# ScalarE's exponential ahead of its PSUM copies, and GpSimd's index copies split in pairs, in a graph network kernel

## The reference, cut to what matters

```
z = (x @ W).reshape(N, H, F)
e = leaky_relu(el[src] + er[dst], 0.2)
m = segment_max(e, dst)
ex = exp(e - m[dst])
s = segment_sum(ex, dst)
out = segment_sum(z[src] * (ex / s[dst]), dst) + b
```

## Time and profile before

| | us |
|---|---|
| median of 3 runs | 7727.45 (7714.45 to 7744.26) |
| the profiled execution | 7731.27 |
| its span, first to last instruction | 7729.6 |
| PE busy | 4457.3 |
| DVE busy | 4150.8 |
| ACT busy | 2129.1 |
| POOL busy | 3270.2 |

### The profile page before, as it was taken

The page is one execution under the profiler, slowest core; times in us unless marked ns, Lnnn a source line. Parts: engine busy times, 40 slices in busy tenths (PEclk is TensorE's granted clock), DMA queues, the critical chain, the costliest instruction groups (busy, mean ns, idle before and its releaser), DMA issues.

```text
span 7729.6 us, 118765 instructions
## 1 busy us (share of the span) xinstructions
PE 4457.3 (58%) x28553; PEld 2928.7 (38%) x28553; DVE 4150.8 (54%) x13273; ACT 2129.1 (28%) x5938; POOL 3270.2 (42%) x3549
## 2 busy tenths in 40 slices
PE   1455555555555565344444444444477988888865
PEld 1223333223233235122222222222256767676754
DVE  3566676767676663455655565556574111223344
ACT  0344444444444441133333233333320000000000
POOL 3666666656565612666666666656600000000000
PEclk9666766666776665566666666666667999999988
DMA  5454454545444532344444444444437989899976
GB/s 88 112 144 134 136 145 131 145 129 145 136 143 134 143 113 49 97 111 122 121 112 121 121 121 116 120 110 123 120 108 287 416 340 416 345 416 401 373 291 260
DMA packets 934339, 1390.68 MB, mean 180 GB/s; under 512 B 483496, under 2 KB 689474, under 8 KB 917769
## 3 DMA queue, kind: packets, MB, share of 16 engines
q1 hardware_dynamic: 687776, 912.42, 35.0%
q0 software_dynamic: 128976, 222.12, 11.6%
q10 hardware_dynamic: 117332, 253.47, 8.8%
HBM read 1014.16 MB, written 373.27 MB: 179 GB/s over the span
## 4 chain that ended last, share of the span: by engine, by line
issue 18%; SPq 16%; PE 14%; another core or an unknown queue 13%; DVE 13%; DMA 13%; ACT 7%; DVEq 4%; ACTq 2%
DMA arena<-adj_w_d 8%; ACT arena L1889 4%; DMA arena<-adj_c_d 4%; SPq L498 4%; SPq L519 4%; PE bank L1754 3%; PE bank L1755 2%; PE bank L1758 2%; SPq L485 2%; DVE arena L1018 2%; PE bank L1716 2%; SPq L500 2%; PE bank L1610 1%; DVE arena L1041 1%
## 5 line engine op out<-in xcount | busy, mean ns | idle before, releaser
L798 POOL DMA_INDIRECT arena<-table_d,arena x3136 | 3093.4, 986 | 1956.7 <-issue 974.0
L1610 PE MATMUL bank<-arena 128*128 128x500 f16 x3750 | 1351.9, 497 | 1312.4 <-issue 720.1
L1631 PE MATMUL bank<-arena 128*65 128x40 f32 x7500 | 649.0, 257 | 1053.8 <-ACT arena L1949 538.8
L1610 PEld LDWEIGHTS bank<-arena 128*128 128x128 f16 x3750 | 430.2, 122 | 2026.1 <-issue 1798.0
L1889 ACT ACTIVATE arena<-arena 128x128 f16<-128x128 f16 x3750 | 1126.6, 392 | 239.1 <-DVEq L1119 133.0
L1631 PEld LDWEIGHTS bank<-arena 128*65 128x65 f32 x7500 | 618.0, 171 | 1174.0 <-issue 611.6
L1754 PE MATMUL bank<-arena 125*128 125x250 f16 x3750 | 857.9, 274 | 156.2 <-DMA arena<-adj_w_d 132.9
L1018 DVE TENSOR_SCALAR arena<-arena 128x500 f16<-128x500 f16 x1875 | 681.7, 364 | 411.5 <-issue 207.2
L1755 PE MATMUL bank<-arena 125*128 125x250 f16 x3750 | 853.9, 273 | 0.0
L1612 PE MATMUL bank<-arena 128*128 128x500 f16 x1875 | 695.7, 474 | 203.6 <-issue 200.1
L1104 DVE SCALAR_TENSOR_TENSOR arena<-arena,bank 128x250 f16<-128x250 f16 x1250 | 455.8, 412 | 559.2 <-ACT arena L1913 297.8
(11 more groups left out here) (244 smaller groups left out, 4244.8 us busy)
## 6 DMA issues: line engine op xcount, KB each, us to landing
arena<-adj_w_d SPq DMA_DIRECT2D x720, 625.0 KB, 10.8
arena<-adj_c_d SPq DMA_DIRECT2D x345, 625.0 KB, 11.4
adj_w_d<-arena ACTq DMA_DIRECT2D x125, 1250.0 KB
arena<-msg_d SPq DMA_DIRECT2D x1250, 103.5 KB
msg_d<-arena POOLq DMA_DIRECT2D x196, 552.0 KB
adj_c_d<-arena ACTq DMA_DIRECT2D x125, 625.0 KB
arena<-table_d,arena POOLq DMA_INDIRECT x3136
arena<-in_edge_features SPq DMA_DIRECT2D x625, 51.0 KB
```

The costliest lines, as they stand in the source:

```text
L798: g_.indirect_dma_start(ring[:, i, k * XC:(k + 1) * XC], None, table_d, bass.IndirectOffsetOnAxis(ap=idx_cur[:, i, k:k + 1], axis=0)).then ...
L1610: mm(wb, lhsT=row_oh[:, slot, c, i, :], rhs=col_oh[:, slot, c, :], start=(c == 0 and i == 0), stop=(c == CH - 1 and i == 1))
L1631: last = mm(out, lhsT=rows_sl[:, g, w, c, 0:AGG], rhs=grh[:, g, w * CH + c, :], start=(c == 0), stop=(c == CH - 1))
```

## The change

In `blocks_pool` the copy of a block's 16 indices becomes 8 copies of two indices, each after the pace wait of its pair and ahead of its two gathers, with a wait for each. In `win_scalar` the wait for `logits_made`, the exponential and its wait come ahead of `finish(g-1)`, and the copies of the first window due go behind that and behind the issue of the maxima's store.

```diff
-                g_.tensor_copy(idx_cur[:, i], row_idx[:, bass.ds(j * BK, BK)]).then_inc(s("idx_here"), 1)
-                wait_reg(pool, s("idx_here"), j + (layer * NBLK + 1))
                 for k in range(BK):
-                    if place is not None and k % 2 == 0:
-                        wait_reg(pool, s("dve_step"), place + k * PER_BLOCK // BK)
+                    if k % 2 == 0:
+                        if place is not None:
+                            wait_reg(pool, s("dve_step"), place + k * PER_BLOCK // BK)
+                        g_.tensor_copy(idx_cur[:, i, k:k + 2], row_idx[:, bass.ds(j * BK + k, 2)]).then_inc(s("idx_here"), 1)
+                        wait_reg(pool, s("idx_here"), j * (BK // 2) + (layer * NBLK * (BK // 2) + k // 2 + 1))
                     g_.indirect_dma_start(ring[:, i, k * XC:(k + 1) * XC], None, table_d, bass.IndirectOffsetOnAxis(
                         ap=idx_cur[:, i, k:k + 1], axis=0)).then_inc(gathered[i], 16)
@@
                     evacuate(b, todo[0] - 1)
+                    act.wait_ge(s("logits_made"), b * NG + (ng + g + 1))
+
+                    wait_some(act, s("win_psum"), b * NG + (ng + g - NG + 1))
+                    act_(flat(grh[:, g]), flat(gd[:, g % GS]), ACT.Exp).then_inc(s("exp_made"), 1)
                     if not (first(b) and g == 0):
                         finish(b if g else b - 1, (g - 1) % NG)
-                    evacuate(b, todo[0])
-                    act.wait_ge(s("logits_made"), b * NG + (ng + g + 1))
-
-                    wait_some(act, s("win_psum"), b * NG + (ng + g - NG + 1))
-                    act_(flat(grh[:, g]), flat(gd[:, g % GS]), ACT.Exp).then_inc(s("exp_made"), 1)
                     act.dma_start(max_d[:, bass.ds((b * NG + g) * (WG * WH), WG * WH)], top_b[0:1, g % 2, 0:WG * WH]).then_inc(top_stored[g % 2], 16)
-                    for n in todo[1:-1]:
+                    for n in todo[:-1]:
                         evacuate(b, n)
```

More of the change, by code:

```diff
@@ L1942, in win_scalar @@
                     evacuate(b, todo[0] - 1)
-                    if not (first(b) and g == 0):
-                        finish(b if g else b - 1, (g - 1) % NG)
-                    evacuate(b, todo[0])
                     act.wait_ge(s("logits_made"), b * NG + (ng + g + 1))
@@ L1949, in win_scalar @@
                     act_(flat(grh[:, g]), flat(gd[:, g % GS]), ACT.Exp).then_inc(s("exp_made"), 1)
+                    if not (first(b) and g == 0):
+                        finish(b if g else b - 1, (g - 1) % NG)
                     act.dma_start(max_d[:, bass.ds((b * NG + g) * (WG * WH), WG * WH)], top_b[0:1, g % 2, 0:WG * WH]).then_inc(top_stored[g % 2], 16)
-                    for n in todo[1:-1]:
+                    for n in todo[:-1]:
                         evacuate(b, n)
```

## The result

The changed kernel takes 7837.3 us (7831.4 to 7843.7) against 7726.9 for the kernel before on the same chip: a ratio of 1.0142, with a 95% interval of 1.0123 to 1.016. It is 110 us slower, where 7680 and 47 us faster was forecast. The profiled execution took 7843.7 us, its span is 7842.0.

The account below looks back on a forecast made before the run. Held signals stretch the VectorE, ScalarE and TensorE loop; after the change GpSimd bounds it. 98 x 26.9 plus a 40 us tail gives 2676 us a stage, -47 and 0, so 7684 profiled, 7680 us median; range 7540 to 8000.

Parts of the forecast that it names:

- What bounds the kernel now: Loop of VectorE, ScalarE and TensorE, stretched by signals held during long gather rows: 21.8 us a group against 17.7 unheld.
- Part one: ScalarE's exponential moved ahead of finish(g-1): taken at -100 us alone, bounds -540 to +250, worth 0 in the sum.
- Part two: GpSimd's index copies in pairs: 5 us more work a block, 26.9 us in all, making GpSimd the bound.
- a tenth up: Upper bound for GpSimd's gap with a copy, 0.1 us above the 1.00 taken: 7840 us.
- The cover: GpSimd's idle time absorbs the added copies: 26.9 us of work a block against 26.8 us taken before.
- The tail: From a stage's last gather to its last logits: 40 us, against 96 and 77.5 before.
- Rival (a): Pauses of 1.0 us free nothing, so signals stay held and the loop slows: 8120 us, chance 0.25.
- The row at 4869.51: In a long gather row, a copy gives 1.08 us without a gather, yet L1910 starts only at 4880.40.
- the row of two gathers: Trace example at 4543.30: after two gathers, the late L1932 starts 0.85 us after the last gather's end.
- Rival (b): GpSimd's pair is 0.1 to 0.2 us cheaper than the rows say: 7400 to 7550 us, chance 0.12.
- Rival (c): Holds come from something other than gathers and GpSimd isn't bound; part one alone pays: 7630 us, chance 0.08.
- The signs: Expected profile marks: 26.9 us a block, VectorE waiting for msg_d, L1932's waits far under 1523 us, tail near 40 us.

Follow-up runs that it names:

- pairs alone: The kernel before with its index copies made two at a time and ScalarE's old order kept: 7817.8 us, ratio 1.011.
- fours: The changed kernel with indices copied four at a time ahead of four gathers: 7218.5 us, ratio 0.9335.
- eights with the long pause: The changed kernel with indices copied eight at a time, each copy made four times over with waits between: 7369.1 us, ratio 0.9552.
- the three forms that ran: The changed kernel with indices copied eight at a time, that copy made two, three or four times over: 7057.8, 7203.4 and 7350.8 us.

## Why the prediction was wrong

**What bounds the kernel now.** Right, and shown: no signal is held over 1.27 us with a quarter of the gathers, nor with memsets for the others, and behind rows of eight a longer pause alone frees them. How the gathers hold them is open. It holds for chips of the slow kind; that the stretch depends on the chip was in no row of the trace that I had.

**Part one.** Right for the sum (its value in it was 0, and pairs alone, 7817.8 us, are within 20 us of both parts). Alone it gives 50 us where 100 was taken. Its bounds, -540 to +250, were far too wide.

**Part two, the step that failed.** "So a block takes 26.9 us when GpSimd never waits." It takes 27.74, so that GpSimd, the bound as forecast, is slower than the 26.8 and 26.5 us of the kernel before and not level with them. The form of the sum is right and its terms are too low by 0.83 us a block: the gathers 16 x 1.010 = 16.16 us against 15.92, 0.24 more; the gaps with a copy, up to 2 us, average 1.014 against 1.00, 0.11 more; the gaps without one average 0.383 with the stores in them, 3.06 us a block against 2.99, 0.07 more; and the 47 gaps over 2 us average 2.72, (2.72 - 1.00) x 47 / 196 = 0.41 more. That is 0.84 x 196 = 164 us; with tails 13 us shorter than taken and 8 us outside the stages it is the 159 us between 7684 and 7843.7. I had taken undisturbed rows for the gap, and a mean of gathers from a kernel in which GpSimd idles a fifth of the time. The mean gather is 986 ns in the kernel before, 997 with fours, 1002 with pairs alone and 1010 in the changed kernel; that the copies and VectorE's traffic stretch it is only argued. The long gap once in four blocks can't be seen in a kernel without eight copies a block; fours have none at that place, and its cause is open. Of the bounds, "a tenth up" for the gap gave 7840, which is where the time came out, but by other terms.

**The cover.** "26.9 against 26.8" left no room: each tenth of a microsecond that the block was underpriced went to the end, 20 us. Forecasting the likelier side from a difference smaller than the error of its terms was the weak point, more than any one row.

**The tail** was taken at 40 us and is 36.6 and 30.6.

**Rival (a)**, that holds stay: it didn't come, and neither did its condition, a pause freeing fewer than one signal in three: behind two gathers it frees 92%. The row at 4869.51 that spoke for it stood behind a long row, and the row of two gathers that spoke against it was the one that carried over. The delay from the start of the aggregate's last matmul to its signal has a median of 0.5 us in the changed kernel and 5.6 in the kernel before; the longest are 4.9 and 35.7, and 3 to 10 us were forecast for the longest holds. **Rival (b)**, the cheaper pair: no, the pair costs more. **Rival (c)**, holds from another source: no, by the two runs with a quarter of the gathers.

**The signs.** VectorE's wait for `msg_d`, L1932's and L1949's waits, the missing pace waits and GpSimd's share came as written, and the gap between pairs is 1.014 us on average (1.07 with the 47 long ones), inside 0.9 to 1.1; VectorE's wait for L1914, L1913 before, is 13.6 us in all, so that part one costs nothing there. Only the block's 26.9 us did not come.

## What to carry to other kernels

An engine's idle time can be what frees the others' signals: before it is filled or trimmed, look for waits that the profile can't name and at what the idle engine was doing when they ended. A pause that frees signals has a price, and what it frees goes by its length and by the row ahead of it; try both as sizes, since here the best of them (four gathers) is 8% faster than the change and its neighbours are not. And where an edit fills an engine to its cover, price it from a loaded stretch and add the rare long gaps, as the middle rows of an idle one are its floor.

## What the runs showed of the hardware

- Long rows of indirect DMAs on GpSimd delay TensorE's semaphore increments, up to 35.7 us from the last matmul's start in the kernel before, and stretch single instructions of SyncE from 29 to 1399 ns. Memsets of 769 ns in a row don't delay the increments (0.91 us at most). Gaps over 1.3 us let 88% (before) and 99% (eights with the long pause) of the pending signals through; those of 1.0 us let 92% through behind two gathers in pairs, 24% behind four and 4% behind eight.
- It isn't on every chip: on two of those used, the kernel before takes 6825 and 6829 us and not 7714 to 7788, and kernels bound by GpSimd take the same within 0.3%. On those two the three forms that ran are slower than the kernel before (7058 to 7351 us), and fours would be by the same sum (7218 against 6825).
- GpSimd's memsets nearly double VectorE's fp16 `tensor_scalar`, 352 to 653 ns; its gathers don't (361 ns).
- A second dependent copy behind a first costs GpSimd 0.2 to 0.3 us and 0.17 us of waiting; from the last copy to a gather it is 0.79 us.
- With eight copies a block GpSimd has a further gap of 1.7 us once in 64 gathers, at the same 47 places in three traces; its cause is open.
